# Decoder layer in two batches: the first unit's row of maxima goes through TensorE and ScalarE instead of four transfers, and six maxima of the second unit stand ahead of the first scores

## The reference, cut to what matters

```python
xn = _layernorm(x, ln_gamma, ln_beta)
q, k, v = proj(w_q), proj(w_k), proj(w_v)
qn = _rmsnorm(q, q_gamma) * dh ** (-0.5)
kn = _rmsnorm(k, k_gamma)
sim = jnp.einsum('bhid,bhjd->bhij', qn, kn)
attn = jax.nn.softmax(sim, axis=-1)
out = jnp.einsum('bhij,bhjd->bhid', attn, v)
```

## Time and profile before

| what | value |
|---|---|
| median of 3 runs | 2412.63 us (2409.85 to 2413.51) |
| the profiled execution: its own time | 2413.03 us |
| its span | 2411.4 us |
| mean granted TensorE clock | 0.962 |
| busy share of the span: PE, ACT, DVE, POOL | 92%, 67%, 64%, 61% |
| instructions | 65807 |

### The profile page before, as it was taken

The page is one execution under the profiler, slowest core; times in us unless marked ns, Lnnn a source line. Parts: engine busy times, 40 slices in busy tenths (PEclk is TensorE's granted clock), DMA queues, the critical chain, the costliest instruction groups (busy, mean ns, idle before and its releaser), DMA issues. The chain is left out here.

```text
span 2411.4 us, 65807 instructions
## 1 busy us (share of the span) xinstructions
PE 2222.3 (92%) x22384; PEld 1264.9 (52%) x22384; DVE 1542.9 (64%) x2599; ACT 1611.7 (67%) x1828; POOL 1481.4 (61%) x978
## 2 busy tenths in 40 slices
PE   6987999999997799899969879999999977998999
PEld 3543666666665345444435436666666653454444
DVE  6986777777773556753269867777777735567532
ACT  3555999999998356631045559999999973566310
POOL 3325888898986566621033259898989865666210
PEclk9997999999999899999979979999999998999999
DMA  4220000000002101100042200000000021011000
GB/s 101 61 40 1 2 9 9 9 9 9 9 9 67 53 2 45 36 18 18 35 107 57 40 1 2 9 9 9 9 9 9 9 67 53 1 45 36 18 18 35
DMA packets 103504, 65.17 MB, mean 27 GB/s; under 512 B 76498, under 2 KB 76498, under 8 KB 103378
## 3 DMA queue, kind: packets, MB, share of 16 engines
q1 hardware_dynamic: 103378, 63.57, 12.3%
HBM read 46.69 MB, written 8.39 MB: 23 GB/s over the span
## 5 line engine op out<-in xcount | busy, mean ns | idle before, releaser
L669 POOL TENSOR_TENSOR probs_l<-probs,probs_h 128x1024 f16<-128x1024 f32 x448 | 979.8, 2214 | 166.5 <-PE bank L721 128.1
L790 DVE TENSOR_REDUCE pm<-bank 128x1 f32<-128x512 f32 x1024 | 680.0, 687 | 277.1 <-PE bank L677 272.6
L773 ACT ACTIVATE probs_h<-bank,shift 128x1024 f16<-128x1024 f32 x512 | 569.0, 1111 | 52.0 <-PE bank L693 52.0
L781 ACT ACTIVATE probs<-bank,shift 128x1024 f32<-128x1024 f32 x512 | 571.7, 1117 | 35.1 <-DVE probs_l L804 30.6
L692 PE MATMUL bank<-q_hh,ko 128*128 (+1 forms) x1024 | 392.0, 383 | 29.5 <-DMA q_lm<-nm 17.0
L677 PE MATMUL bank<-ko,q_hh 128*128 (+1 forms) x1024 | 397.1, 391 | 20.8 <-PEq L314 12.3
L693 PE MATMUL bank<-q_lm,k_h 65*128 (+1 forms) x1024 | 392.1, 383 | 0.0
L706 PEld LDWEIGHTS bank<-v_hl,probs_h 128*128 128x128 f16 x4096 | 288.3, 98 | 66.3 <-issue 8.1
L706 PE MATMUL bank<-v_hl,probs_h 128*128 (+1 forms) x4096 | 321.0, 192 | 0.8 <-ACT probs_h L773 0.8
L708 PE MATMUL bank<-v_hl,probs_h 128*128 (+1 forms) x4096 | 318.9, 193 | 0.0
L708 PEld LDWEIGHTS bank<-v_hl,probs_h 128*128 128x128 f16 x4096 | 268.2, 96 | 59.1 <-issue 0.6
(11 more groups left out here) (230 smaller groups left out, 4201.3 us busy)
## 6 DMA issues: line engine op xcount, KB each, us to landing
xt_a<-in_x SPq DMA_DIRECT2D x32, 256.0 KB, 2.6
q_lm<-in_x SPq DMA_DIRECT2D x32, 256.0 KB, 4.5
ko<-in_L_ffn_W SPq DMA_DIRECT2D x32, 256.0 KB, 3.8
q_hh<-q_hh SPq DMA_DIRECT2D x32, 128.0 KB, 2.5
ko<-k_h SPq DMA_DIRECT2D x32, 128.0 KB, 2.7
q_lm<-nm SPq DMA_DIRECT2D x256, 0.2 KB, 4.9
out<-bo_b SPq DMA_DIRECT2D x16, 256.0 KB, 2.0
out<-xbo_b SPq DMA_DIRECT2D x16, 256.0 KB, 2.0
```

What stands on the lines that cost most here:

```text
L669: pool.tensor_tensor(probs_l[:, p % 2, :], probs[:, p % 2, :], probs_h[:, p % 4, :], ALU.subtract).then_inc(pl_pool, 1)
L773: act.activation(probs_h[:, p % 4, :], SB[p % 2][:, :], ACT.Exp, bias=shift[:, 0:1]).then_inc(ph_ready, 1)
L781: act.activation(probs[:, p % 2, :], SB[p % 2][:, :], ACT.Exp, bias=shift[:, 0:1]).then_inc(p_ready, 1)
L790: dve.tensor_reduce(pm[:, s, k:k + 1], MB[k % 2], AX_X, ALU.max).then_inc(mx_free, 1)
```

## The change

It has four parts.

1. The row of unit 0 (of each batch, so twice per launch) is not sent by SP. `negate_max(0, 0)` writes into the last column of a zeroed tile `nm0` (128 x 4 x 65, f16). Four products of `nm0[:, a, :]` (128x65, stationary) with an f16 identity `eye16` (128x128) put the numbers in row 64 of a bank of the output pair (`OB[0]`), and ACT copies that row of 512 into row 64 of `q_lm` and adds 64 to `m_ready`. SP's loop begins at unit 1.
2. For that, POOL zeroes `nm0` at the head of the block, DVE makes `eye16` from `ident` before its first reduction, and three semaphores order them.
3. Six maxima of unit 1 (`AHEAD = 6`), products and reductions, stand ahead of `scores(0, 0)`: two before the four small products, four behind. Steps 0 and 1 of unit 0 skip them (step 0 has no maxima, step 1 has two).
4. The memset of row 64 of `k_h1` moves from the head of the self-attention block to POOL's head in the first block.

```diff
@@ POOL, first block
+                        pool.memset(k_h1[DH:DH + 1, :, :].rearrange("p h n -> p (h n)").bitcast(F32), TWO_ONES)\
+                            .then_inc(a_ones, 1)
+                        pool.wait_ge(a_ones, 2 * b + 1)
+                        pool.nop(nofuse=True)
                         pool.wait_ge(a_const, 32 * (b + 1))
@@ self-attention block
+                    eye16 = sb(ph, "eye16", [P, P], F16)
+                    nm0 = sb(ph, "nm0", [P, TPC, DH + 1], F16)
+                    AHEAD = 6
@@ SP
-                        for r in range(UNITS):
+                        for r in range(1, UNITS):
@@ POOL
+                        pool.memset(nm0[:, :, :], 0.0).then_inc(e_zero, 1)
                         pool.memset(v_hl[:, :].rearrange("p (k e) -> p k e", e=VW)[:, :, DH:DH + 1], 1.0)\
-                            .then_inc(a_ones, 1)
-                        pool.wait_ge(a_ones, 2 * b + 1)
-                        pool.nop(nofuse=True)
-                        pool.memset(k_h1[DH:DH + 1, :, :].rearrange("p h n -> p (h n)").bitcast(F32), TWO_ONES)\
                             .then_inc(a_ones, 1)
@@ PE, unit
                                         for k in range(2):
-                                            unit_max(1 + p // 4, p % 4 * 4 + half * 2 + k)
+                                            if p * 4 + half * 2 + k >= AHEAD:
+                                                unit_max(1 + p // 4, p % 4 * 4 + half * 2 + k)
@@ PE
                         for k in range(16):
                             unit_max(0, k)
+                        for k in range(2):
+                            unit_max(1, k)
+
+                        pe.wait_ge(e_eye, b + 1)
+                        pe.wait_ge(nm_ready, U0 + 3)
+                        pe.nop(nofuse=True)
+                        for a in range(TPC):
+                            mm = pe.matmul(OB[0][0:DH + 1, a * P:(a + 1) * P], nm0[:, a, :], eye16[:, :],
+                                           start=True, stop=True)
+                        mm.then_inc(e_row, 1)
+                        for k in range(2, AHEAD):
+                            unit_max(1, k)
                         pe.wait_ge(a_ones, 2 * b + 2)
                         scores(0, 0, fresh=True)
@@ ACT
                         act.preload_act_table(ACT.Exp)
+                        act.wait_ge(e_row, b + 1)
+                        act.activation(lf[DH:DH + 1, 0:CT], OB[0][DH:DH + 1, :], ACT.Copy).then_inc(m_ready, ROW)
@@ DVE, negate_max
-                            dve.tensor_reduce(nm[:, s, :], pm[:, s, :].rearrange("p (a k) -> p a k", k=4), AX_X, ALU.max,
+                            dve.tensor_reduce(nm0[:, :, DH] if isinstance(r, int) and r == 0 else nm[:, s, :], pm[:, s, :].rearrange("p (a k) -> p a k", k=4), AX_X, ALU.max,
                                               negate=True).then_inc(nm_ready, 1)
@@ DVE, unit
-                                for k in range(16):
+                                for k in range(AHEAD, 16):
                                     reduce_max(1, k, 1)
@@ DVE
+                        dve.tensor_copy(eye16[:, :], ident[:, :]).then_inc(e_eye, 1)
                         for k in range(16):
                             reduce_max(0, k, 0)
+                        dve.wait_ge(e_zero, b + 1)
                         negate_max(0, 0)
+                        for k in range(AHEAD):
+                            reduce_max(1, k, 1)
                         unit(0, 0, first=True)
```

More of the change, by code:

```diff
@@ L193, in decoder_layer @@
         a_dup = sem("a_dup")
+        e_row = sem("e_row")
+        e_zero = sem("e_zero")
+        e_eye = sem("e_eye")
         s_ready = sem("s_ready")
```

## The result

| | median, us | runs |
|---|---|---|
| before | 2412.40 | 6, 2406.47 to 2413.69 |
| changed | 2395.67 | 6, 2393.23 to 2399.46 |
| ratio | 0.9936, 95% interval 0.9923 to 0.9949 | |

The change is faster by 15.4 us by the ratio (12 to 19 with the interval), 16.7 by the medians. The forecast was 2401.6 with a range from 2397.0 to 2406.0: the direction is right, and the gain is larger than the range allowed.

A forecast was written before the change was run, and what follows sets the result against it. PE, busy 92% of the span, was the bound; its first self-attention scores waited 17.0 us for transfers of `nm`. 3.9 + 1.6 + 0.5 - 0.5 = 5.5 us per batch, 11.0 for two, gave 2401.6 us; range 2397.0 to 2406.0.

The forecast's parts named there:

- The row: Self-attention's head, first batch: products and ACT's copy replace the 7.5 us path by transfers; row ready at 194.6, bounds 194.2 to 195.9.
- T: Start of self-attention's first scores in a batch: from 200.44 to 196.5, 3.9 us earlier, bounds 196.1 to 197.1.
- Step 0: First step of unit 0, losing all four maxima: ACT sets its end, 4.2 us after the first scores; gain 1.6 us.
- The maxima hide the row: Ahead of the first scores: the row, ready at 194.6, is hidden by the six maxima by 1.9 us.
- The memset costs nothing: POOL's head in the first block: the moved memset of 6.92 us ends at about 13.1, before POOL's first work at 14.94.
- the cover: First block, both batches: 1.8 us between the moved memset's end and POOL's first work; each us beyond delays the batch by up to one.
- The four transfers gone, the cast and the small memset are small: Head of self-attention: these small things were all put at nothing, the bound being 0.3 us each.
- step 2 of the change: Unit 0's step 2: clock rises at 205.5, 9.0 us after the first scores as before; step takes 3.6 us, loss 0.5.
- step 1: Unit 0's step 1, losing two maxima: 3.4 us at half clock against 3.95 before, gain 0.5 us.
- The four terms: Per batch, first scores' move, step 0, step 1 and step 2: 3.9 + 1.6 + 0.5 - 0.5 = 5.5 us earlier.
- the clock rises early: Rival, chance 0.20: at self-attention's head the clock rises at 200.6; 7.4 us per batch, 2397.8 us.
- Only the row is won: Rival, chance 0.07: steps 0 and 1 keep their length, so 3.9 us per batch remain, 2404.8 us.

The follow-up runs named there:

- row_only: The changed kernel with no maxima of unit 1 ahead of the first scores, the row still by products and ACT's copy: 2397.62 us, ratio 0.9940 to before.
- fill_ahead2: The changed kernel plus unread products behind the first block and each unit 0 maximum, two maxima ahead, four in step 0: 2387.18 us, ratio 0.9886 to before.
- ahead_only: The changed kernel with the row sent by SP's four transfers as before, six maxima still ahead: 2406.28 us, ratio 0.9971 to before.
- fill_lead: The changed kernel plus one unread product behind each of the four maxima between the small products and the first scores: 2392.90 us, ratio 0.9919 to before.
- fill_only: The changed kernel plus one unread product behind each of unit 0's 16 maxima, none behind the first block: 2392.15 us, ratio 0.9910 to before.
- ahead12: The changed kernel with twelve maxima of unit 1 ahead in place of six: 2400.94 us, ratio 0.9951 to before.
- memset_back: The changed kernel with the memset of row 64 of k_h1 back at the head of self-attention: 2397.76 us, ratio 0.9940 to before.
- warm24_fill: The changed kernel plus 24 unread products behind the first block's last transposes and one behind each of unit 0's 16 maxima: 2391.79 us, ratio 0.9915 to before.
- warm24: The changed kernel plus 24 unread products on PE behind the last transposes of the first block: 2393.40 us, ratio 0.9931 to before.

## Why the prediction was wrong in size

**Right.** The row was ready 13.85 us after the head (193.80; foreseen 194.6, or 13.8 after a head at 180.77). T came at 15.55 after the head against 15.7. Step 0 came out as reasoned from ACT: T to the scores of pair 0.2 took 4.12 us for a foreseen 4.2, gain 1.7 for 1.6. The maxima hide the row, and with all of them gone (row_only) or four of the six (fill_ahead2) the row itself sets T. The memset costs nothing (with it the first block took 173.94 and 174.92 us, before 174.68 and 175.44), and its price beyond the cover is at least as stated, though the cover of the second batch is only 0.75 us in the profiled execution, where I took it to be the same as the first's 1.8. The four transfers gone, the cast and the small memset are small; the cast is not nothing but 0.2 us. There the rule of the Trainium skill (SBUF — State Buffer, Who interferes with whom), which the prediction left out of the sum, fits: a cast beside memsets took 0.95 and 0.35 us, 0.22 alone. The longer one ends at 180.94, right behind POOL's second memset (180.86), the shorter at 179.96, right behind the first (179.88).

**Wrong.** The step that failed is in step 2 of the change: "With the same delay it now rises at 205.5". The delay behind the first scores is not a property that the scores carry with them. The rise came 2.5 to 3.3 us behind them in four heads of the changed kernel. That makes step 1 ACT's 2.0 us instead of 3.4 (gain 1.9 for 0.5) and step 2 3.1 instead of 3.6 (loss 0 for 0.5). The four terms are then 4.1 + 1.7 + 1.9 + 0 = 7.7 per batch for the 5.5 forecast; it is the rival "the clock rises early", priced at 7.4, to which I gave 0.20. I weighed against it that before the rise took 9.0 us "with short waits between maxima", and for it that the first two pairs now run in one piece. Neither argument decides it. A pause ahead of the scores went with the late rise in every head (the kernel before, row_only, ahead_only), and products in the gaps of the maxima with one before the scores (fill_lead, fill_only). But ahead12 has the same first two pairs in one piece right behind a maximum and rose 8.9 us behind T, and memset_back did both in one execution. So what makes the rise early in nine heads of ten of the kernels with the short row and six maxima ahead stays open, and in a single head it is in part luck. The late batch of memset_back meets the forecast's 5.5 only as a sum: there T gains 4.3 (forecast 3.9), step 0 1.7 (1.6), step 1 0.6 (0.5), and step 2 loses 1.1 (0.5), with the rise at +10.4 and not +9.0.

**Not weighed: the row without the maxima.** "Only the row is won", at 3.9 us per batch, kept the six maxima ahead and let them win nothing; that did not come, since steps 0 and 1 shrank in every kernel with six maxima ahead. The row with no maxima ahead I did not price: there T comes at 13.88, 5.8 us earlier, more than my forecast for the whole change. The six maxima ahead then win only through the clock: with a late rise the kernel with them has s(1,1) at 43.04, without them 42.70, and with an early one 40.75.

**Not settled.** Outside the two heads the profiled executions differ by several us. Cross-attention took 266.1 and 266.6 us in the profiled execution of the kernel before and 262.5 to 267.7 elsewhere (263.1 and 266.4 in the kernel before again), with the mean granted clock there between 0.92 and 0.94: its own rises and falls of the clock come out differently by batch. By the medians row_only gains 4 us, ahead_only 4.5 and ahead12 5 us more than their heads explain, the change 1 us. So a part of each ratio is not owed to the edit's place, and why the kernel before lies at the slow end in every set of runs is open; no run aimed at it. It matters for the range: the 15.6 us of the two heads alone, taken from 2412.6, give 2397.1, just inside it; the rest puts the measured 2395.7 below.

## What to carry to other kernels

A few numbers that must turn from a column into a row are turned by TensorE and ScalarE in 1.5 us, where four small transfers took 7.5; with nothing between, that won nearly the full difference (5.8 of 6.0 us per batch, row_only). Work moved ahead of a start is paid there, so it wins only where it fills a wait: the six maxima won 1.2 us per batch in the wait for the transfers (ahead_only); with the short row they won 2.0 where the clock rose early and lost 0.3 where it rose late. Where the granted clock is at half in a serial stretch, compute the gain for both places of the rise, and look whether products whose results nobody reads can hold it; that was worth 2.6 us per batch at the two heads (warm24_fill).

## What the runs showed of the hardware that I had not expected

The full clock fell 1.7 us behind the head after two pauses of no more than 1.0 us each (warm24), and did not come back in 14 us of maxima at one in 0.7 us; one unread product more per maximum held it over the same stretch, across the same first pause of 0.98 us and a second of 0.55 us (warm24_fill). A stretch of 3.40 us with one pause of 0.19 us passed at half clock (the change), and so did 4.4 us with none behind the first scores of the kernel before, while in fill_lead the clock rose at 195.23, 2.7 us after the start of the small products at 192.55. And with T at 15.36 in both batches of one execution, the rise came at +2.4 and at +10.4, which is worth 2.5 us (memset_back).
